# Attention kernel on one core: the masked product of keys and values leaves VectorE, and the linear product moves one slot later on TensorE

## What is computed

```
q = layernorm(q); k = layernorm(k)                       # per head, 8 channels
aw  = softmax(q k^T / sqrt(8));  kth = 12th largest of each row
o_s = (aw where aw >= kth, normalised) @ v               # sparse part
qf  = softmax(q, channels);  kf = softmax(k, channels)
kv  = einsum('bhnd,bhne->bhde', kf, v)                   # 8x8 per head
z   = einsum('bhnd,bhd->bhn', qf, kf.sum(tokens))
o_l = einsum('bhnd,bhde->bhne', qf, kv) / (z + 1e-6)     # linear part
out = x + (a * o_s + (1 - a) * o_l) @ Wproj.T + bproj + xn @ W[idx] + b[idx]
```

## Time and profile before

| | |
|---|---|
| three runs | 1179.04, 1184.93, 1180.96 us; median 1180.96 |
| the profiled execution | 1181.1 us, of which the span of its instructions is 1179.3 |
| busy share of the span | DVE 97%, ACT 90%, POOL 84%, PE 80%, PEld 55% |
| DMA | 68 GB/s over the span |

### The profile page before, as it was taken

How to read it: one execution, slowest core, us unless ns; L and a number is a source line. 1 busy time by engine, 2 the same in 40 slices (tenths; PEclk the granted TensorE clock), 3 DMA queues, 4 the chain that set the end, 5 groups by cost and what they waited for, 6 DMA issues and landing times.

```text
span 1179.3 us, 34136 instructions
## 1 busy us (share of the span) xinstructions
PE 942.5 (80%) x9061; PEld 653.6 (55%) x9092; DVE 1148.9 (97%) x4358; ACT 1063.5 (90%) x3474; POOL 995.5 (84%) x1973
## 2 busy tenths in 40 slices
PE   4578878888888888888888888888887888888887
PEld 1355556555555555555555555555555555555555
DVE  7999999999999999999999999999999999999997
ACT  3689989999999999999999999999999989999986
POOL 6688888888889888889888888888888888889865
PEclk9999999999999999999999999999999999999999
DMA  3112321223321222231223231223221223321220
GB/s 100 46 55 82 86 86 38 77 61 86 87 84 39 70 68 86 86 87 37 77 60 86 86 86 45 70 59 86 86 86 48 67 61 86 86 82 38 71 63 13
DMA packets 165122, 82.74 MB, mean 70 GB/s; under 512 B 7737, under 2 KB 164927, under 8 KB 164930
## 3 DMA queue, kind: packets, MB, share of 16 engines
q1 hardware_dynamic: 164658, 80.43, 23.8%
q10 hardware_dynamic: 272, 0.13, 0.0%
HBM read 42.78 MB, written 37.75 MB: 68 GB/s over the span
## 4 chain that ended last, share of the span: by engine, by line
POOL 30%; ACT 24%; issue 18%; PE 17%; DVE 10%; DVEq 1%; POOLq 0%; DMA 0%; ACTq 0%; SPq 0%
ACT e L881 14%; POOL gap L439 10%; POOL below L443 5%; DVE top L656 4%; PE work_ps L1155 3%; DVE rest L663 3%; POOL qkn L361 3%; PE turn_ps L1051 3%; PE pv_ps L1073 3%; POOL qk_b L361 3%; POOL drop L414 2%; PE work_ps L1143 2%; POOL sq_half L424 2%; ACT part L910 2%; PE work_ps L1186 2%
## 5 line engine op out<-in xcount | busy, mean ns | idle before, releaser
L881 ACT ACTIVATE e<-score_ps,drop 128x256 f32<-128x256 f32 x1024 | 474.6, 492 | 32.3 <-POOL drop L414 32.2
L1051 PE MATMUL turn_ps<-ident,e 128*128 128x128 f32 x2016 | 382.9, 284 | 40.1 <-ACT kept L841 20.5
L663 DVE MATCH_REPLACE8 rest<-e 128x256 f32<-128x256 f32 x1020 | 411.6, 407 | 0.0
L669 DVE MAX8 next<-rest 128x8 f32<-128x256 f32 x1020 | 405.7, 413 | 0.5 <-issue 0.3
L656 DVE MAX8 top<-score_ps 128x8 f32<-128x256 f32 x1024 | 360.0, 413 | 10.2 <-PE score_ps L1033 10.0
L439 POOL TENSOR_SCALAR gap<-e,next 128x256 bf16<-128x256 f32 x794 | 368.9, 479 | 0.1
L1052 PE MATMUL turn_ps<-minus_huge,below 128*128 128x128 bf16 x2016 | 363.1, 221 | 0.0
L1051 PEld LDWEIGHTS turn_ps<-ident,e 128*128 128x128 f32 x2016 | 286.6, 142 | 72.4 <-issue 44.1
L841 ACT ACTIVATE kept<-turn_ps 128x1024 f32<-128x1024 f32 x252 | 266.9, 1059 | 36.6 <-PE turn_ps L1052 36.6
L443 POOL TENSOR_SCALAR below<-gap 128x768 bf16<-128x768 bf16 (+1 forms) x254 | 216.7, 853 | 41.7 <-POOL gap L439 41.7
L881 ACT ACTIVATION_READ_ACCUMULATOR e<-score_ps,drop 128x1 f32 x1024 | 230.6, 225 | 0.0
(11 more groups left out here) (229 smaller groups left out, 1398.3 us busy)
## 6 DMA issues: line engine op xcount, KB each, us to landing
part_slots<-part SPq DMA_DIRECT2D x128, 192.0 KB, 2.3
q_slots<-part_slots SPq DMA_DIRECT2D x64, 256.0 KB, 3.4
k_slots<-part_slots SPq DMA_DIRECT2D x64, 256.0 KB, 3.9
part_slots<-part SPq DMA_DIRECT2D x64, 128.0 KB, 1.9
x_sb<-in_L_attn_x SPq DMA_DIRECT2D x32, 128.0 KB, 3.9
x_res<-in_L_attn_x SPq DMA_DIRECT2D x32, 128.0 KB, 4.0
out_y<-out_sb SPq DMA_DIRECT2D x32, 128.0 KB, 4.1
w_ops<-in_L_ffn_W SPq DMA_DIRECT2D x1, 512.0 KB
```

The lines of the kernel that those rows point to most:

```text
L663: nc.vector.match_replace(rest[:, t, :], e8[:, (u_ - 1) % 2, t, :], e[:, (u_ - 1) % RING, t, :], REMOVED).then_inc(s["rest_ready"], 1)
L669: nc.vector.max(next8[:, (u_ - 1) % RING, t, :], rest[:, t, :]).then_inc(s["next_ready"], 1)
L881: nc.scalar.activation(e[:, u_ % RING, t, :], score_ps[:, u_ % 2, t // 2, t % 2, :], ACT.Exp, bias=drop[:, u_ % 2, t, 0:1], accum_out=z[:, ...
L1051: mm(dst, e[:, r, t, keys], ident[:], start=True, stop=False, is_transpose=True)
```

## The change

ACT copies the product of keys and values from PSUM into a new buffer `kv_raw` at the end of u1. POOL masks it into `kv` in u2, right behind drop(2); DVE has no part in it any more. On PE the linear product moves from the end of u2 to u3, behind the turn and ahead of the rest of that slot. On ACT the copy of its result moves from ahead of e(3) to behind it.

```
 POOL, u_ == 2, behind drop:
+  if it == 0:
+      pool.wait_ge(s["head_ready"], 1)
+  pool.wait_ge(s["kv_copied"], it + 1)
+  nc.gpsimd.tensor_tensor(kv[:], kv_raw[:], own_head[:], ALU.mult).then_inc(s["kv_ready"], 1)
 DVE, u_ == 2:
-  dve.wait_ge(s["w_kv"], it + 1)
-  nc.vector.tensor_tensor(kv[:], work_ps[:, 0:H * VA].rearrange("p (h e) -> p h e", e=VA),
-                          own_head[:], ALU.mult).then_inc(s["kv_ready"], 1)
 ACT, behind e and e8:
+  if u_ == 1 and exists(it):
+      act.wait_ge(s["w_kv"], it + 1)
+      wait(act, s["kv_ready"], it)
+      nc.scalar.copy(kv_raw[:].rearrange("p h e -> p (h e)"), work_ps[:, 0:H * VA]).then_inc(s["kv_copied"], 1)
 ACT, u_ == 3, from ahead of e to behind e8:
   act.wait_ge(s["w_lin"], it + 1)
   wait(act, s["lin_ready"], it)
   nc.scalar.copy(lin_raw.rearrange("p g e -> p (g e)"), work_ps[:, 0:NT * H * VA]).then_inc(s["lin_copied"], 1)
 PE, the linear product, from late(2) to u3 between turn(3) and early(3):
-  if u_ == 2 and exists(it):            # in late, behind the scores
+  if u_ == 3 and exists(it): linear()   # behind turn and product, ahead of early
```

More of the change, by code:

```diff
@@ L169, in build @@
         v_aug = sb("v_aug", [P, 2, NT, H, VW])
+        kv_raw = sb("kv_raw", [P, H, VA])
         kv = sb("kv", [P, H, VA])
@@ L212, in build @@
             dmax_ready dsub_ready dexp_ready ksum_step ksum_ready over_logs over_ready feat_ready
-            w_v_ready v_copied w_kv kv_ready w_qfT qfT_copied w_lin lin_copied lin_ready
+            w_v_ready v_copied w_kv kv_copied kv_ready w_qfT qfT_copied w_lin lin_copied lin_ready
             w_turn sums_copied eps_ready osp_ready w_osT osT_copied w_out y_ready""".split()
@@ L428, in body @@
                         shift(it)
+                    if u_ == 2 and exists(it):
+                        if it == 0:
+                            pool.wait_ge(s["head_ready"], 1)
+                        pool.wait_ge(s["kv_copied"], it + 1)
+                        nc.gpsimd.tensor_tensor(kv[:], kv_raw[:], own_head[:], ALU.mult).then_inc(s["kv_ready"], 1)
                     if u_ == 2 and it >= 0 and exists(it + 1):
@@ L671, in extra @@
                 def extra(u_, k):
-                    if u_ == 2 and k == 1 and exists(it):
-                        if it == 0:
-                            dve.wait_ge(s["head_ready"], 1)
-                        dve.wait_ge(s["w_kv"], it + 1)
-                        nc.vector.tensor_tensor(kv[:], work_ps[:, 0:H * VA].rearrange("p (h e) -> p h e", e=VA),
-                                                own_head[:], ALU.mult).then_inc(s["kv_ready"], 1)
                     if u_ == 3 and k == 5 and it >= 0 and exists(it + 1):
@@ L855, in body @@
                         rsqrt_steps(it)
[L856 to L860, removed]
                     if u_ == 4 and exists(it + 1):
@@ L886, in body @@
                         nc.scalar.activation(e8[:, u_ % 2], drop[:, u_ % 2, :, 1:9], ACT.Exp).then_inc(s["e8_ready"], 1)
+                    if u_ == 1 and exists(it):
+                        act.wait_ge(s["w_kv"], it + 1)
+                        wait(act, s["kv_ready"], it)
+                        nc.scalar.copy(kv_raw[:].rearrange("p h e -> p (h e)"), work_ps[:, 0:H * VA]).then_inc(
+                            s["kv_copied"], 1)
+                    if u_ == 3 and exists(it):
+                        act.wait_ge(s["w_lin"], it + 1)
+                        wait(act, s["lin_ready"], it)
+                        nc.scalar.copy(lin_raw.rearrange("p g e -> p (g e)"), work_ps[:, 0:NT * H * VA]).then_inc(
+                            s["lin_copied"], 1)
                     if u_ in (0, 4) and exists(it - 1):
@@ L1097, in remainder, with linear @@
                        stop=True, skip_group_check=True).then_inc(s["w_rest"], 1)
+                def linear():
+                    pe.wait_ge(s["kv_ready"], it + 1)
+                    for t in range(NT):
+                        last = mm(work_ps[:, t * H * VA:(t + 1) * H * VA], qfT[:, t * P:(t + 1) * P],
+                                  kv[:].rearrange("p h e -> p (h e)"), start=True, stop=True)
+                    last.then_inc(s["w_lin"], 1)
                 def early(u_):
@@ L1171, in late @@
                         last.then_inc(s["w_kv"], 1)
-                    if u_ == 2 and exists(it):
[L1174 to L1178, removed]
                     if u_ == 3 and exists(it + 1):
@@ L1227, in body @@
                         sums()
+                    if u_ == 3 and exists(it):
+                        linear()
                     early(u_)
```

## The result

The changed kernel takes 1251.01 us (median of four runs, 1249.47 to 1252.56) against 1181.8 for the kernel before in the same runs: a ratio of 1.0579, 95% interval 1.0558 to 1.0600. It is 69.2 us slower; 1250 was forecast.

What follows compares the result with a forecast made beforehand. The prediction took a slack-free chain of waits through DVE, POOL, PE and ACT, as long as DVE's own work, as the bound. 1181.1 + 48.7 (later `w_qkT`) + 20 (PE's clock) = 1250 us, range 1222.6 to 1272.

Steps and rivals of the forecast that it cites:

- The ring: Closed chain of waits DVE, POOL, PE, ACT, PE, ACT, DVE through a 35.07 us batch, claimed to have no slack.
- e8: ACT's step that DVE's removal in u7 needs; for batch step 6 it ends 0.17 us before that removal starts.
- The delay of `w_qkT`: On PE, `w_qkT` starts 1.57 us later, 0.43 from POOL's mask and 1.14 from ACT's order; 48.7 us over 31 batches.
- The order on ACT: Copying the linear product behind e(3) makes `w_qkT` wait for that copy instead of `qkn`: 1.14 us a batch.
- One to one: A delay of `w_qkT` or the turn behind it lengthens the batch by the same amount.
- The clock: PE's longer wait ahead of `w_qkT` lets its clock fall: 0.65 us a batch, between 0 and 1.29; 20 us in all.
- the rival in which the clock stays up: Only the later `w_qkT` costs time, PE staying at full rate: 1230 us, 22% chance.
- the case of 1270 us: PE's clock falls fully in each of 31 batches, adding 1.29 us each to the 1.57: 1270 us, 22% chance.
- What was costed at nothing: ACT's copy to `kv_raw` in u1 and PE's moved linear product were claimed to fit in idle time: cost nothing.
- The mask taken off DVE: DVE loses 0.22 us 32 times, 7.0 us, but waits that much longer for e8 in u7: worth nothing.
- The DMAs: Transfers to DRAM and back feeding the next batch's first scores shift by as much as DVE does: nothing added.
- signs to look for: `w_qkT` waits for ACT's copy; DVE's e8 waits grow about as the batch; batches 36.6 to 37.9 us; DVE busy 7 to 9 less.

Runs made afterwards that it cites:

- the filler: Changed kernel with 26 small matmuls of constants on PE ahead of `w_qkT`, in its wait: 1229.73 us, ratio 1.0385.
- the copy put back: Changed kernel with ACT copying the linear product ahead of e(3) again, as in the kernel before: 1203.87 us, ratio 1.0154.
- the copy's place alone: Kernel before with only ACT's copy of the linear product moved behind e(3); mask and product stay as they were: 1245.12 us, ratio 1.0520.
- the copy put back and `qk_exp` in u5: Changed kernel with ACT copying the linear product ahead of e(3) and its exponentials of q and k moved from u4 to u5: 1183.81 us, ratio 1.0006.
- the kernel before with `qk_exp` in u5: Kernel before with ACT's exponentials of q and k moved from u4 to u5: 1173.49 us, ratio 0.9920.
- the fastest one: Changed kernel, linear product copied ahead of e(3), `qk_exp` in u5, one of POOL's marked tiles in u2 given to ACT: 1167.23 us, ratio 0.9865.

## Why the prediction was right

**The ring.** Right. It closes with e8(6) and the removal in u7, 0.17 us apart as before; shortening it by a step that the change leaves alone shortens the changed kernel's batch and makes the kernel before faster.

**The delay of `w_qkT`.** 1.57 us were worked out, 1.49 measured. The mask moved what is behind it by 0.44 (0.43 forecast; it lasts 0.49, not 0.47). The order on ACT cost 1.05, not 1.14: PE starts 0.05 us after the copy's end at 918.08, where I had taken the 0.14 that it took behind POOL. The batch grew by 1.54.

**One to one.** Right in a clean batch: 1.49 at `w_qkT`, 1.55 at the removal, 1.54 in the batch.

**The clock.** 0.65 us a batch were chosen between 0 and 1.29; the whole is (69.2 − 47.7) / 31 = 0.69, the filler gives 21 us back, and the 1229.73 us with it are the 1230 of the rival in which the clock stays up. The size was right; that the half came so near was luck. Its reason was a fall that comes late and slows only what is left. The trace has a fall near `w_qkT` in 16 batches, 15 more than before, and 12 of them begin ahead of it; if these account for all of it, 21.5 / 15 makes about 1.4 us for each, an estimate that is near the full price of 1.29. So it was about half of the batches at the full price, not all at half of it, nor all 31 at the full price, the case of 1270 us. Where the falls do come late they seem cheaper: with the copy put back 11 of 12 begin behind the start of `w_qkT`, and 6 us are lost. And I read a wait of 1.45 us as one that leaves the clock alone: in the run with the copy put back waits of 1.31 us end at either level, and with the copy's place alone shorter waits than in the changed kernel cost more, 28 us. The length of that one wait doesn't decide by itself. How often the clock falls, nothing here foretells.

**What was costed at nothing.** The copy to `kv_raw` and the move on PE: right, the move by a run of its own, the copy by the clean batch with the copy put back and by ACT's idle time ahead of e(2), which shrinks from 0.82 to 0.28 us and still covers it. The mask taken off DVE: right as long as the ring is the longer one (with the copy put back and `qk_exp` in u5 DVE idles 34.99 − 34.77 = 0.22 us of a clean batch), and its 0.22 us show as soon as it isn't. The DMAs: no term was needed.

**A path that was not seen.** The prediction lets a fall of the clock reach DVE by `kept` and e8(6) alone. DVE's wait for scores grew from 10.0 to 35.3 us, and 22.3 us of these lie 4 to 8 us behind a `w_qkT`, as in the row at 848.66, where the slow PE is late with the next slot's scores; with filler none are left there. So in those batches the delay reaches DVE earlier than at the removal.

**Wrong in signs to look for.** DVE's waits for e8 were to grow by as much as the batch; they grew by 38 us, and those for scores by 25. Batches were to last up to 37.9 us where the clock falls; 14 of the last 29 were longer, most of them up to 38.8. DVE's busy time was to fall by 7 to 9 us; it rose from 1148.9 to 1153.4, with 32 instructions less. Neighbouring instructions of DVE overlap, busy time counts an overlap once, and an added wait takes an overlap away; that this makes up the difference was not measured. It fits that between two runs with few waits, the kernel before with `qk_exp` in u5 and the fastest one, the busy time falls by 6.9 us, from 1146.5 to 1139.6.

## What to carry to other kernels

An engine at 97% can stand beside a ring of waits of the same length; then taking work off that engine is worth nothing until the ring is shorter, and an instruction moved behind others on a less busy engine can be paid in full. Look for the ring by following one late instruction through a batch that differs from the others; the place to relieve is any step on it, also one that has nothing to do with the change. Moving a copy out of another engine's way needs a look at who waits for the copy, above all where a PSUM bank is handed from step to step.

## What was not expected of the hardware

Identical waits of 2.33 us end with TensorE at 2.4 GHz in one batch and at 1.2 GHz in another of the same execution. And 26 matmuls without use in each batch made a kernel 21 us faster; the mean granted clock went from 0.953 to 0.989.
